# A four-layer decoder kernel: weight loads moved into the layernorm ahead of each sublayer, a wait per array in the latent attention's folds, gathered feed-forward rows issued one sublayer earlier

## The reference

```
x = x + L0_attn(layernorm(x))         # linear attention with decay, 16 heads
x = x + L0_xattn(layernorm(x), ctx)   # causal attention over 256 context rows, 16 heads of 16
x = x + L0_ffn(layernorm(x))          # gated feed-forward, rounded to fp8, columns picked by index lists
x = x + L1_attn(layernorm(x))         # selective state-space scan
x = x + L1_xattn(layernorm(x), ctx)   # latent attention over 512 context rows
x = x + L1_ffn(layernorm(x))          # 8 experts, the best 2 of each token
x = x + L2_attn(layernorm(x))         # gated delta rule
x = x + L2_xattn(layernorm(x), ctx)   # latent attention
x = x + L2_ffn(layernorm(x))          # gated, 2 of 4 kept
x = x + L3_attn(layernorm(x))         # differential attention
x = x + L3_xattn(layernorm(x), ctx)   # latent attention
x = x + L3_ffn(layernorm(x))          # shared expert and 8 experts of 176
```

```python
q_hk = (hidden_q @ Wq.T).reshape(b, s, H, K)            # H = 16, K = 128
q_big = jnp.einsum('bshk,hkq->bshq', q_hk, w_kc_q)      # 192 per head
q_r = jnp.einsum('bshq,hqr->bhsr', q_big, W_qr)         # 64 per head
k_r = jnp.einsum('bld,hdr->bhlr', kv_rope, W_kr)
attn = jax.nn.softmax(jnp.einsum('bhsr,bhlr->bhsl', q_r, k_r), axis=-1)
ctx_lat = jnp.einsum('bhsd,hkd->bshk', jnp.einsum('bhsl,bld->bhsd', attn, kv_rope), w_kc_kv)
out = ctx_lat.reshape(b, s, H * K) @ Wo.T
```

## Time and profile before

| | |
|---|---|
| runs | 3569.09, 3573.97, 3584.52 us |
| the profiled execution, its own time | 3572.01 us |
| its span, first to last instruction | 3570.2 us |
| mean granted TensorE clock | 0.803 |
| busy: PE | 2707.2 us, 76% |
| busy: DVE | 1797.3 us, 50% |
| busy: ACT | 981.6 us, 27% |
| busy: POOL | 800.4 us, 22% |
| read from HBM | 65.04 MB, 20 GB/s over the span |

### The profile page before, as it was taken

One profiled execution on the slowest core, in us unless ns is written; L12 is line 12 of the kernel. 1 busy time (PEld: TensorE's weight loads), 2 busy tenths in 40 slices (PEclk: granted clock), 3 DMA queues, 4 the chain that ended last, 5 costly groups with the idle time before them and its releaser, 6 DMA issues. The chain is left out here.

```text
span 3570.2 us, 37436 instructions
## 1 busy us (share of the span) xinstructions
PE 2707.2 (76%) x14214; PEld 1752.2 (49%) x14214; DVE 1797.3 (50%) x3596; ACT 981.6 (27%) x2209; POOL 800.4 (22%) x565
## 2 busy tenths in 40 slices
PE   4799434265799998967786878659997764799799
PEld 2545322122333555545666766555555633555555
DVE  5422468698233555238475656532564654155511
ACT  2121101153000554113434333322553111155311
POOL 0000200022000885310000000001883000088422
PEclk8765655566899998978797878777998865799899
DMA  1000100000200001021000000030000001100211
GB/s 38 6 10 1 33 1 1 3 0 26 62 0 0 1 1 41 9 96 24 1 12 13 12 13 12 13 83 0 1 1 36 1 17 53 30 1 1 74 48 39
DMA packets 96634, 72.72 MB, mean 20 GB/s; under 512 B 51248, under 2 KB 89952, under 8 KB 95881
## 3 DMA queue, kind: packets, MB, share of 16 engines
q1 hardware_dynamic: 95433, 68.88, 6.9%
q0 software_dynamic: 1024, 1.45, 0.2%
HBM read 65.04 MB, written 5.28 MB: 20 GB/s over the span
## 5 line engine op out<-in xcount | busy, mean ns | idle before, releaser
L1890 POOL TENSOR_SCALAR work<-work,small 128x512 f32<-128x512 f32 x384 | 593.1, 1562 | 1000.2 <-DVE small L1826 1000.2
L1868 ACT ACTIVATE work<-psum,small 128x512 f32<-128x512 f32 x384 | 260.2, 683 | 252.1 <-DVE small L1821 252.1
L1821 DVE TENSOR_REDUCE small<-psum 128x2 f32<-128x1024 f32 x192 | 234.9, 1225 | 179.2 <-PE psum L1771 179.2
L1771 PE MATMUL psum<-keysT,arena_a 64*128 64x512 f32 x768 | 219.0, 649 | 9.1 <-ACT work L1868 6.2
L1781 PEld LDWEIGHTS psum<-consts,work 128*128 128x128 f32 x1536 | 165.9, 142 | 113.5 <-issue 103.9
L1793 PE MATMUL psum<-work,keys 128*64 128x256 f32 x1536 | 187.0, 384 | 36.8 <-issue 34.0
L1781 PE MATMUL psum<-consts,work 128*128 128x128 f32 x1536 | 211.8, 281 | 3.2 <-DVE work L1832 2.6
L1793 PEld LDWEIGHTS psum<-work,keys 128*64 128x64 f32 x1536 | 120.0, 137 | 136.5 <-issue 110.6
L2684 PE MATMUL psum<-xnT,arena_a 128*128 128x256 f32 x512 | 152.3, 458 | 30.2 <-DVE arena_b L3064 30.2
L1425 PE MATMUL psum<-arena_b,arena_a 96*96 96x512 f32 x128 | 94.2, 907 | 71.4 <-DVE arena_b L1454 37.0
L2684 PEld LDWEIGHTS psum<-xnT,arena_a 128*128 128x128 f32 x512 | 115.8, 234 | 56.1 <-DVE arena_b L3064 32.6
(11 more groups left out here) (576 smaller groups left out, 5148.6 us busy)
## 6 DMA issues: line engine op xcount, KB each, us to landing
arena_a<-in_L_xattn_Wo SPq DMA_DIRECT2D x3, 2048.0 KB, 12.4
arena_a<-in_L_xattn_Wq SPq DMA_DIRECT2D x3, 2048.0 KB, 15.0
arena_a<-in_L_xattn_w_kc_q SPq DMA_DIRECT2D x3, 1536.0 KB, 20.1
arena_a<-in_L_attn_w_qkv SPq DMA_DIRECT2D x1, 4096.0 KB
arena_a<-in_L_xattn_W_qr SPq DMA_DIRECT2D x3, 768.0 KB, 4.5
arena_b<-in_L_ffn_w_fc SPq DMA_DIRECT2D x1, 2048.0 KB
arena_b<-in_L_ffn_w_proj SPq DMA_DIRECT2D x1, 2048.0 KB
arena_a<-in_L_attn_w_gate SPq DMA_DIRECT2D x1, 2048.0 KB
```

Of the source, the lines that this page charges most:

```text
L1771: mm = nc.tensor.matmul(ps[:, u % 2 * 2 + j, :], qT[r:r + DC, p, t * P:(t + 1) * P], k.keysT[r:r + DC, b * SK:(b + 1) * SK], start=True, s ...
L1821: nc.vector.tensor_reduce(top[:, 2 * u:2 * u + 2], ps[:, u % 2 * 2:u % 2 * 2 + 2, :], AX.X, ALU.max, negate=True).then_inc(*maxed.up())
L1868: nc.scalar.activation(probs[u % NPB][:, j, :], ps[:, u % 2 * 2 + j, :], ACT.Exp, bias=top[:, i:i + 1], accum_out=total[:, i:i + 1]).then_ ...
L1890: nc.gpsimd.tensor_scalar(probs[u % NPB][:, j, :], probs[u % NPB][:, j, :], total[:, i:i + 1], None, ALU.mult).then_inc(*scaled.up())
```

## The change

1. Every sublayer becomes a generator. Up to its `yield` it carves its arrays and defines `fetch`, the loads; `program` hands that to the layernorm, whose SP stream issues them, and lets the rest run behind it.
2. The latent attention's single name is split. `W_qr`, `W_kr` ("first") and `w_kc_kv`, `Wo` ("second") are loaded in the layernorm; `w_kc_q` ("third"), `Wq` ("fourth") and L1's tables ("fifth") still in the sublayer's first block, now with `w_kc_q` ahead of `Wq`. Each fold waits for its own arrays; the tables are waited for by DVE in the block after.
3. The lists as columns are loaded in the layernorm of L0_xattn, into `small`, and POOL issues the 24 indirect DMAs of L0_ffn at the end of its stream in L0_xattn's first block, into the upper part of `arena_b`, which L0_xattn leaves free.
4. L3_ffn keeps only the shared expert's loads in the layernorm; the eight experts' loads stand in the SP stream of its own block.

The diff, cut. The other sublayers' loads move as those of L0_xattn do.

```diff
@@ l0_xattn
+    def fetch(sp):
+        load(k, sp, "first", [(wq, interleaved(io["L0_xattn_Wq"])), (wkv, io["L0_xattn_Wkv_expand"]),
+                              (hide, k.const("hide")), (one_row, k.const("one_row")),
+                              (ctxT, io["ctxT"].rearrange("d (b s) -> d b s", b=B)),
+                              (wo, interleaved(io["L0_xattn_Wout"]))])
+        l0_ffn_columns(k, sp)
+
+    yield fetch
     with k.block() as block:
-
-        @block.sync
-        def _(sp):
-            load(k, sp, "first", [(wq, interleaved(io["L0_xattn_Wq"])), (wkv, io["L0_xattn_Wkv_expand"]),
...
             nc.gpsimd.memset(vz[:, :, 16:17], 1.0).then_inc(*prep.up())
+            l0_ffn_gather(k, pool)
@@ new functions
+def l0_ffn_gathered(k):
+    F, FT = 704, 8
+    FP = F // FT
+    up_col, down_col, down2 = (carve(k.small, 448 + 8 * i, parts, n, dt=I32) for i, (parts, n) in
+                               enumerate(((P, 2), (FP, FT), (FP, FT))))
+    return up_col, down_col, down2, carve(k.arena_b.t, 8192, FP, 2 * FT, D)
+def l0_ffn_gather(k, pool):
+    nc, gathered = k.nc, k.sig("gathered")
+    _, down_col, down2, wgu = l0_ffn_gathered(k)
+    FT = down_col.shape[1]
+    k.wait_weights(pool, "columns")
+    for t in range(FT):
+        nc.gpsimd.indirect_dma_start(down2[:, t:t + 1], None, k.io["down_table"],
+                                     bass.IndirectOffsetOnAxis(ap=down_col[:, t:t + 1], axis=0)).then_inc(*gathered.up(16))
+    pool.wait_ge(gathered.sem, gathered.total)
+    for g, name in enumerate(("L0_ffn_w_gate", "L0_ffn_w_up")):
+        for t in range(FT):
+            nc.gpsimd.indirect_dma_start(wgu[:, g * FT + t, :], None, k.io[name], bass.IndirectOffsetOnAxis(
+                ap=down2[:, t:t + 1], axis=0)).then_inc(*gathered.up(16))
@@ latent_attention
+    def fetch(sp):
+        load(k, sp, "first", [(w_qr, io[n + "W_qr"]), (w_kr, io[n + "W_kr"])])
+        load(k, sp, "second", [(w_v, io[n + "w_kc_kv"].rearrange("h k d -> k h d")),
+                               (wo, io[n + "Wo"].rearrange("(h k) o -> k h o", h=H))])
+
+    yield fetch
     with k.block() as block:
 
         @block.sync
         def _(sp):
-            load(k, sp, tag, [(w_qr, io[n + "W_qr"]), (w_kr, io[n + "W_kr"]),
...
+            load(k, sp, "third", [(w_qc, io[n + "w_kc_q"].rearrange("h k q -> k h q") if rope else
+                                   io[n + "w_kc_q"].rearrange("h (c q) k -> q h c k", c=2))])
+            load(k, sp, "fourth", [(wq, io[n + "Wq"].rearrange("(h k) i -> k h i", h=H))])
+            if rope:
+                load(k, sp, "fifth", [(sin, k.const("q_sin")[0:QH].rearrange("p (c s) -> p c s", c=2)),
+                                      (cos, k.const("q_cos")[0:QH].rearrange("p (c s) -> p c s", c=2))])
...
-            k.wait_weights(pe, tag)
+            k.wait_weights(pe, "first")
...
+            k.wait_weights(pe, "second")
             for h in range(H):
...
@@ l3_ffn
         @block.sync
         def _(sp):
+            own_gate_up(sp, "fourth", 0, 3)
+            load(k, sp, "third", [(down[64:P, 5, :], own_down[0:64, :]), (down[:, 6:16, :], rows(own_down[64:64 + 1280, :])),
+                                  (down[0:64, 16, :], own_down[64 + 1280:, :])])
+            own_gate_up(sp, "fifth", 3, E)
             sp.wait_ge(*kept.at(2))
@@ program
         for stage in STAGES:
-            layernorm(k, interleave=stage in ("L0_attn", "L0_xattn"), fetch=FETCH[stage](k) if stage in FETCH else None)
-            if stage in SUBLAYERS:
-                SUBLAYERS[stage](k)
-            else:
-                latent_attention(k, stage)
+            sublayer = SUBLAYERS[stage](k) if stage in SUBLAYERS else latent_attention(k, stage)
+            layernorm(k, interleave=stage in ("L0_attn", "L0_xattn"), fetch=next(sublayer))
+            next(sublayer, None)
```

239 lines of the change are left out of this document (105 added, 134 removed).

## The result

| | before | changed |
|---|---|---|
| median of the runs side by side | 3571.53 us (4 runs, 3527.39 to 3584.52) | 3423.25 us (4 runs, 3370.08 to 3434.57) |
| profiled execution, its own time | 3572.01 us | 3433.46 us |
| its span | 3570.2 us | 3431.6 us |

The account below looks back on a forecast made before the run. Loads came in bursts after each layernorm, a 10.5 us slot without transfers, while PE waited on DMAs. Sublayer gains summed to 150.7 us off the profiled 3572.0, giving 3421.3; with the median 2 us above, 3423 us, range 3402 to 3444.

Parts of the forecast that it names:

- The slot: Every layernorm: 10.5 us in which no transfer runs; with loads issued in it, it still lasts 10.5 us.
- The gathered rows: L0_ffn: DVE's 18.89 us wait for gathered rows goes, and the gather costs nothing in L0_xattn.
- L0_attn: First sublayer: of DVE's 4.35 us wait for its tables 3.8 goes; gain taken as 2.5 us, bounds 1.5 and 3.8.
- L2_attn: First block: POOL's scaling of w_out starts earlier but holds DVE's scans until its end; gain 6.6 us, bounds 2.9 and 10.6.
- L1_xattn, L2_xattn, L3_xattn: Latent sublayers: third folds start earlier, gaining 22.3 us in L1_xattn and 27.1 each in L2_xattn and L3_xattn.
- Rival 3: Transfers give time back: L1611's race lost, POOL holds DVE, openings lose clock; 25 to 30 us less gain, 3450; chance 0.10.
- no wait of PE on a DMA over 4 us at a fold: Sign that the forecast is right: at the folds, PE waits on no DMA for more than 4 us.
- L0_xattn: Block's opening: POOL's 6.94 us wait before the copies PE needs goes, a gain of 6.9 us.
- rival 1: L0_xattn's loop: the clock stays up, some 12 units save 4.5 us each, 55 us more gain, 3368; chance 0.05.
- a PEclk row unlike the one before in L0_xattn: Sign that the forecast is wrong: PE's granted clock in L0_xattn differs from the kernel before.

## Why the prediction held, and where it did not

**The slot.** That a layernorm with loads still lasts 10.5 us held in every sublayer: first matmuls come 10.6 us behind its start in L2_xattn, L2_ffn, L3_attn and L3_ffn. The terms that rest on it, in L0_ffn together with the gathered rows, came out within 1.1 us each: L0_ffn 26.3 for 25.8, L1_ffn 4.4 for 4.0, L2_ffn 10.6 for 10.5, L3_attn 9.7 for 8.6, L3_ffn 9.7 for 9.3.

**The gathered rows.** 18.9 us were said to go; 19.5 came back when the gather did. That they cost nothing in L0_xattn was not quite right: in five of seven profiles signals came late there, at 2.2 us in the pair that has a price, 5.3 at most in another.

**L0_attn.** 5.3 for 2.5, above the upper bound of 3.8. DVE's table was held up by POOL's scaling by 0.3 us only (it was POOL that was slower, 3.49 us where it took 1.82), so ACT starts 3.7 us earlier. The rest is spread: this sublayer, the same in all, took 131.3 to 140.2 us in the eleven profiles of the changed kernel and its variants.

**L2_attn.** 6.9 for 6.6 looks exact, and the mechanism is the one given: two runs show that POOL's instruction holds DVE's, and which ones. But the agreement is in part luck. The term is about the first block, and the next one starts 40.0 us behind the layernorm's start where it started 1595.95 - 1547.49 = 48.5: 8.4 us, 1.8 more than forecast. POOL's instruction started where it was said to, 26.9 us behind the layernorm's start. What was wrong is that all eight scans would run behind its end: the first was let go before it, and they ended 0.75 us behind it and not 2.62. The batches behind then took 1.5 us longer than before, which is within their spread. The next block's first row, before and changed:

```profile
1595.95 0.64 DVE L3051 COPY eye<-consts 128x128 f32<-128x128 f32 x4 [10.21 <-PEq L72]
1533.37 0.63 DVE L3071 COPY eye<-consts 128x128 f32<-128x128 f32 x4 [0.30 <-PEq L72]
```

**L1_xattn, L2_xattn, L3_xattn.** The third folds started 21.5 us earlier in L1_xattn (22.3 forecast) and 26.1 in L2_xattn (27.1): the landing was 0.8 to 1 us later than worked out. The step that failed is the silent one behind it, that a fold takes what it took. It does only at the same clock: 13.92 us at a mean 0.50 for 9.60 at 0.75, and 13.44 at 0.79 for 10.67 at 1.00, while what follows gave 1 to 2 back. The terms were too high by 2.6, 3.5 and 3.2 us. Rival 3 had named lost clock in the openings. The same step failed the other way in the first two folds of L2_xattn, which took 6.7 us at 1.00 and not 10.6; so the third stood waiting, and the sign "no wait of PE on a DMA over 4 us at a fold" did not come: 5.49 us in L2_xattn, 5.29 in L1_xattn, 4.29 in L3_xattn.

**L0_xattn.** The step that failed stands in rival 1: "the four executions of before agree within 16 us, so the fall is no matter of luck." The fall is not, but the rise is, and the next execution of the kernel before took 3527.4 us, 42 below the four. The fall comes at the loop's start; the rise came 17 to 188 us later in the ten profiles with that fall, and 17 and 184 in the very same program. The forecast took the clock of one execution as a property of the kernel. The ±30 us that this adds to any single execution are larger than every bound of the sum, and that the median met the forecast's 3423 is luck, by the mix of its four executions: 3370, 3413, 3433, 3435. The later rise is also the sign that the prediction had put under "wrong", a PEclk row unlike the one before in L0_xattn. Without L0_xattn the profiled executions show a gain of 141.3 us (138.5 with the changed kernel's second profile) for 143.8 forecast, and that is the part which the sum can claim; even there the 9.3 us missing in the latent sublayers are made up in part by gains of 6.7 above the forecast elsewhere.

What stays open: what brings the clock down at the start of L0_xattn's loop, the pause or the thin work around it; what brings it up again after a time that differs between executions of one program; why the latent folds run at 0.50 even without a wait; and by which way the signals between engines come late while indirect DMAs run, and whether they do so without the profiler.

## What to carry to other kernels

A stage boundary in which no transfer runs is worth its full length to every stage whose first use waits at least that long for a load, and it is read from two rows: SP's first issue and the first wait that it ends. Order loads by first use and, where the arithmetic allows it, the uses by the size of their loads; name each array's landing. Before a median is compared with a sum, look at what the same program does twice: a stage that may run at either clock is a term with a spread, and some added matmuls where the clock falls may settle it (12 here, for 11 us of PE).
